# MoE stages with routed experts: units on gathered rows, planned on the core, results added in the stage that follows

## The reference

```python
probs = sigmoid(xt @ gate_w.T + gate_b)
w, idx = top_k(probs, 2)
w = w / (sum(w) + 1e-08)
for e in range(6):
    h = silu(xt @ ew1[e].T) * (xt @ ew3[e].T)
    y = y + ge[:, e:e + 1] * (h @ ew2[e].T)     # ge is w, and zero for four of the six experts
z = silu(xt @ fc1.T) * (xt @ fc2.T) @ fc3.T
x = x + 0.5 * (y + z)                            # xt is layernorm(x)
```

## Time and profile before

| | |
|---|---|
| median of 3 runs | 4698.61 us (4684.21 to 4701.09) |
| the profiled execution | 4671.09 us |
| its span, first to last instruction | 4669.5 us |
| PE, DVE, ACT, POOL busy | 91%, 64%, 49%, 15% |
| mean granted TensorE clock | 0.942 of full |
| moved by DMA | 359.15 MB |

### The profile page before, as it was taken

How to read it: one execution, slowest core, us unless ns; L and a number is a source line. 1 busy time by engine, 2 the same in 40 slices (tenths; PEclk the granted TensorE clock), 3 DMA queues, 4 the chain that set the end, 5 groups by cost and what they waited for, 6 DMA issues and landing times. The chain is left out here.

```text
span 4669.5 us, 79371 instructions
## 1 busy us (share of the span) xinstructions
PE 4239.2 (91%) x25648; PEld 2522.6 (54%) x25648; DVE 3004.6 (64%) x5513; ACT 2295.4 (49%) x4375; POOL 682.8 (15%) x698
## 2 busy tenths in 40 slices
PE   7999969999999999986999989639999999997688
PEld 6888743333333333324888855525656656654454
DVE  5556668888888888835656533746666666663432
ACT  3222317777777777761332222214656556655222
POOL 2232200000000000000233200532222222220000
PEclk9999979999999999987999999868999989998789
DMA  2000172323323322203000000476667667662401
GB/s 85 0 0 0 52 146 38 46 34 43 46 34 44 46 38 39 32 6 120 8 0 0 1 20 0 150 198 179 188 176 184 188 165 186 191 158 52 131 20 36
DMA packets 173944, 359.15 MB, mean 77 GB/s; under 512 B 40586, under 2 KB 104714, under 8 KB 156810
## 3 DMA queue, kind: packets, MB, share of 16 engines
q1 hardware_dynamic: 154634, 304.20, 28.5%
q0 software_dynamic: 18944, 50.35, 3.9%
HBM read 209.71 MB, written 152.06 MB: 77 GB/s over the span
## 5 line engine op out<-in xcount | busy, mean ns | idle before, releaser
L1314 DVE TENSOR_REDUCE full_tops<-psum 128x1 f32<-128x1024 f32 x1024 | 1206.2, 1218 | 184.0 <-PE psum L1218 184.0
L1271 ACT ACTIVATE full_probs<-psum 128x512 f32<-128x512 f32 x2048 | 1065.8, 602 | 299.2 <-PE psum L1190 295.1
L1781 ACT ACTIVATE causal_probs<-psum 128x512 f32<-128x512 f32 (+3 forms) x1280 | 640.2, 533 | 397.9 <-PE psum L1653 230.0
L1190 PE MATMUL psum<-full_q,full_k 49*128 49x512 f32 x2048 | 653.3, 475 | 23.2 <-ACT full_probs L1271 17.2
L1832 DVE TENSOR_REDUCE causal_tops<-psum 128x1 f32<-128x1024 f32 (+7 forms) x704 | 586.8, 857 | 112.6 <-PE psum L1704 112.6
L1190 PEld LDWEIGHTS psum<-full_q,full_k 49*128 49x128 f32 x2048 | 284.5, 186 | 605.8 <-ACT full_probs L1271 576.9
L1199 PE MATMUL psum<-full_probs,full_vh 128*32 128x512 f32 x4096 | 556.8, 616 | 0.7 <-ACT full_probs L1271 0.7
L1218 PE MATMUL psum<-full_k,full_q 48*128 48x512 f32 x2048 | 402.0, 458 | 51.4 <-DMA full_k<-qk_split 23.6
L1653 PE MATMUL psum<-causal_q,causal_k 49*128 49x512 f32 (+3 forms) x1280 | 407.7, 451 | 14.2 <-ACT causal_probs L1781 8.3
L1704 PE MATMUL psum<-causal_k,causal_q 48*128 48x512 f32 (+4 forms) x1152 | 325.3, 414 | 70.2 <-DVE causal_tops L1847 33.4
L274 POOL TENSOR_TENSOR moe_h_lo<-moe_h,moe_h_hi 128x512 fp32r<-128x512 f32 x224 | 290.3, 1296 | 661.2 <-ACT moe_h_hi L387 661.2
(11 more groups left out here) (190 smaller groups left out, 6070.7 us busy)
## 6 DMA issues: line engine op xcount, KB each, us to landing
causal_bias<-bias_tiles SPq DMA_DIRECT2D x32, 1280.0 KB, 6.3
band_scores<-xn POOLq DMA_DIRECT2D x256, 160.0 KB, 4.2
...
```

The lines of the kernel that those rows point to most:

```text
L1190: nc.tensor.matmul(k.psum[:, b, :], k_sb[at, q, kt * P:(kt + 1) * P], q_sb[at, q, n * BLK:(n + 1) * BLK], start=True, stop=True).then_inc( ...
L1271: nc.scalar.activation(pT[:, kt % 4, n * BLK:(n + 1) * BLK], k.psum[:, bank(q, u), :], ACT.Exp).then_inc(p_ready, 1)
L1314: nc.vector.reduce_max(mx[:, q % 2, u // 2, u % 2:u % 2 + 1], src, AX_X).then_inc(m_free, 1)
L1781: nc.scalar.activation(dst, k.psum[:, bank(q, u), 0:(hi - lo) * P], ACT.Exp).then_inc(p_ready, 1)
```

## The change: what it does, and the diff

`moe_then` joins a MoE stage with the stage after it. The MoE stage now has 29 units: for v = 0 to 7 the shared expert on the 8 blocks, then `NX` = 21 units of 512 gathered rows, each of one expert.

- Beside the shared units, DVE chooses two experts a token (`choose`, `weigh`), PE counts with small matmuls how many tokens before this one took the same expert (`positions`), and DVE makes slot numbers of it (`locate`). SP stores the normalized rows to DRAM (`XN`). POOL scatters the token numbers to their slots (`scatter`, 8 indirect DMAs of 128 numbers a block). The gate's matmuls are now float32r parts too.
- After the last block DVE plans the units (`schedule`): for each of the 21 its expert and where its token numbers stand. SP reads the plan and loads weights and numbers of each unit (`load_weights`, `load_ids`); POOL gathers the rows (`gather`, 4 indirect DMAs of 128 rows of 1 KB a unit), four units ahead.
- In an expert unit the rows are transposed and split like x, the weights are split per unit (`split` on ACT, `rest` on DVE), and the result is copied by ACT (`out`) and stored by SP to DRAM (`YS`), not added to x.
- `Returns`: in the following stage POOL gathers for each tile its two result rows per token (`pool_bring`), and DVE adds them with their weights (`dve_add`) ahead of the statistics.
- The first MoE stage no longer waits for all of x; `load_stage` gives each quarter a semaphore and ends with the identity. The loops of the MoE, qkv and LSTM stages that carry new work are unrolled where these need it.

`positions` is six small float32 matmuls a block; `locate` is 13 DVE operations on at most 24 columns, `schedule` 14 on at most 105.

```diff
-STAGES = [moe(0), full_attention, moe(1), lstm(0), causal_attention, lstm(1)]
+ROW_ORDER = list(range(TT))
+PAIR_ORDER = [t * (TT // NB) + n * TB + i for n in range(TT // NB // TB) for t in range(NB) for i in range(TB)]
+STAGES = [moe_then(0, ROW_ORDER, full_attention), moe_then(1, PAIR_ORDER, lstm(0)), causal_attention, lstm(1)]
...
+NX = 16 + E - 1
...
+                def load_weights(b):
+                    if b >= 2:
+                        sp.wait_ge(w_lo, b - 1)
+                    at = sp.value_load(plan[0:1, 0, b:b + 1], min_val=0, max_val=E - 1)
+                    sp.dma_start(w_raw[:, w_slot(NBLK + b), :],
+                                 experts[:, bass.ds(at, 1), :].rearrange("p a x -> p (a x)")).then_inc(s_raw[w_slot(NBLK + b)], 16)
+
+                def load_ids(b):
+                    if b >= 6:
+                        sp.wait_ge(k.gathered[(b - 6) % 4], gathered(b - 6))
+                    at = sp.value_load(plan[0:1, 1, b:b + 1], min_val=0, max_val=HOME - 1)
+                    sp.dma_start(idr[:, b % 6, :], ids[bass.ds(at, 1)].rearrange("a p t -> (a p) t")).then_inc(s_id[b % 6], 16)
+
+                def store(b):
+                    sp.wait_ge(y_copied, 2 * b + 2)
+                    sp.dma_start(outs[b], ybuf[:, b % 2, :, :].rearrange("p t d -> p (t d)")).then_inc(s_y[b % 2], 16)
+
+                sp.wait_ge(plan_ready, 1)
+                for b in range(2):
+                    load_weights(b)
+                sp.wait_ge(k.scattered, scattered_all())
+                for b in range(4):
+                    load_ids(b)
+                load_weights(2)
+                for v in range(NBLK, NV + 1):
+                    if v >= NBLK + 1:
+                        store(v - NBLK - 1)
+                    if v - 5 < NX:
+                        load_weights(v - 5)
+                    if v - 4 < NX:
+                        load_ids(v - 4)
...
+                def scatter(n):
+                    pool.wait_ge(idx_ready, n + 1)
+                    for t in range(n * TB, (n + 1) * TB):
+                        for s in range(2):
+                            pool.indirect_dma_start(
+                                out=k.TOKENS[:, :], out_offset=bass.IndirectOffsetOnAxis(ap=idx[:, s, t:t + 1], axis=0),
+                                in_=token[:, t:t + 1], in_offset=None).then_inc(k.scattered, 16)
+
+                def gather(b):
+                    pool.wait_ge(s_id[b % 6], 16 * (b // 6 + 1))
+                    if b >= 4:
+                        pool.wait_ge(t_ready, 2 * (NBLK + b - 4) + 2)
+                    if b == 0:
+                        for r in range(2):
+                            pool.wait_ge(s_xn[r], 16 * NBLK // 2)
+                    for t in range(TB):
+                        pool.indirect_dma_start(
+                            out=xg[:, b % 4, t, :], out_offset=None, in_=k.XN[:, :],
+                            in_offset=bass.IndirectOffsetOnAxis(ap=idr[:, b % 6, t:t + 1], axis=0)).then_inc(k.gathered[b % 4], 16)
...
+                for v in range(NBLK - 2):
+                    rest(v + 1, 0)
+                    rest(v + 1, 1)
+                    if v + 4 < NBLK:
+                        ln.pool_rstd(pool, v + 4, v % 2)
+                    scatter(v + 1)
+                rest(NBLK - 1, 0)
+                rest(NBLK - 1, 1)
+                scatter(NBLK - 1)
+                for b in range(4):
+                    gather(b)
+                rest(NBLK, 0)
+                rest(NBLK, 1)
+                for v in range(NBLK, NV - 1):
+                    rest(v + 1, 0)
+                    if v - 4 < NX:
+                        gather(v - 4)
+                    rest(v + 1, 1)
...
+                for v in range(NBLK - 2):
+                    up(v + 1, 0, (0,))
+                    positions(v + 1)
+                    up(v + 1, 0, (1,))
+                    transpose(v + 2)
+                    up(v + 1, 1)
+                    gate(v + 2)
+                    down(v, 0)
+                    gate_transpose(v + 2)
+                    down(v, 1)
+                up(NBLK - 1, 0, (0,))
+                positions(NBLK - 1)
+                up(NBLK - 1, 0, (1,))
+                up(NBLK - 1, 1)
+                for v in (NBLK - 2, NBLK - 1):
+                    down(v, 0)
+                    down(v, 1)
+                transpose(NBLK)
+                transpose(NBLK + 1)
+                up(NBLK, 0)
+                up(NBLK, 1)
+                for v in range(NBLK, NV):
+                    if v + 1 < NV:
+                        up(v + 1, 0)
+                    if v + 2 < NV:
+                        transpose(v + 2)
+                    if v + 1 < NV:
+                        up(v + 1, 1)
+                    down(v, 0)
+                    down(v, 1)
...
+                def split(b):
+                    r = w_slot(NBLK + b)
+                    if b >= 2:
+                        act.wait_ge(dn_ready, 2 * (NBLK + b - 3) + 2)
+                    act.wait_ge(s_raw[r], 16 * (b // 3 + 1))
+                    nc.scalar.copy(w_parts[0][:, r, :], w_raw[:, r, :]).then_inc(w_hi, 1)
+
+                def out(b, pair):
+                    act.wait_ge(dn_ready, 2 * (NBLK + b) + pair + 1)
+                    if b >= 2 and pair == 0:
+                        act.wait_ge(s_y[b % 2], 16 * (b // 2))
+                    nc.scalar.copy(ybuf[:, b % 2, 2 * pair:2 * pair + 2, :].rearrange("p t d -> p (t d)"),
+                                   k.psum[:, 4 + pair, :]).then_inc(y_copied, 1)
...
+                for v in range(NBLK, NV):
+                    if v + 1 < NV:
+                        hidden(v + 1, 0)
+                    if v + 2 < NV:
+                        upper_x(v + 2)
+                    if v + 1 < NV:
+                        hidden(v + 1, 1)
+                    out(v - NBLK, 0)
+                    out(v - NBLK, 1)
+                    if v + 3 < NV:
+                        split(v + 3 - NBLK)
...
+                for v in range(NBLK - 2):
+                    locate(v + 1)
+                    hidden(v + 1, 0)
+                    lower_x(v + 2)
+                    if v + 3 < NBLK:
+                        apply(v + 3)
+                    hidden(v + 1, 1)
+                    choose(v + 2)
+                    weigh(v + 2)
+                    update(v)
+                    if v + 4 < NBLK:
+                        stats(v + 4)
+                locate(NBLK - 1)
+                schedule()
+                hidden(NBLK - 1, 0)
+                hidden(NBLK - 1, 1)
+                update(NBLK - 2)
+                rest(1)
+                rest(2)
+                update(NBLK - 1)
+                lower_x(NBLK)
+                lower_x(NBLK + 1)
+                rest(3)
+                hidden(NBLK, 0)
+                hidden(NBLK, 1)
+                address()
+                for v in range(NBLK, NV):
+                    if v + 1 < NV:
+                        hidden(v + 1, 0)
+                    if v + 2 < NV:
+                        lower_x(v + 2)
+                    if v + 1 < NV:
+                        hidden(v + 1, 1)
+                    if v + 3 < NV:
+                        rest(v + 4 - NBLK)
...
+    def pool_bring(self, pool, first, count):
+        k = self.k
+        for i in range(first, first + count):
+            if i >= 8:
+                pool.wait_ge(k.added, self.run * TT + i - 7)
+            g = self.order[i]
+            for s in range(2):
+                pool.indirect_dma_start(
+                    out=self.ring[:, i % 8, s, :], out_offset=None, in_=k.YS[:, :],
+                    in_offset=bass.IndirectOffsetOnAxis(ap=self.back[:, s, g:g + 1], axis=0)).then_inc(k.back[i % 8], 16)
+
+    def dve_add(self, dve, first, count):
+        k, nc = self.k, self.k.nc
+        for i in range(first, first + count):
+            dve.wait_ge(k.back[i % 8], 32 * (self.run * TT // 8 + i // 8 + 1))
+            g = self.order[i]
+            nc.vector.scalar_tensor_tensor(k.X[:, g, :], self.ring[:, i % 8, 0, :], self.wgt[:, 0, g:g + 1], k.X[:, g, :],
+                                           ALU.mult, ALU.add).then_inc(k.added_half, 1)
+        for i in range(first, first + count):
+            dve.wait_ge(k.added_half, self.run * TT + i + 1)
+            g = self.order[i]
+            nc.vector.scalar_tensor_tensor(k.X[:, g, :], self.ring[:, i % 8, 1, :], self.wgt[:, 1, g:g + 1], k.X[:, g, :],
+                                           ALU.mult, ALU.add).then_inc(k.added, 1)
...
             @block.gpsimd
             def _(pool):
+                ret.pool_bring(pool, 0, 2 * TB)
                 ln.pool_rstd(pool, 0, 0)
+                ret.pool_bring(pool, 2 * TB, TB)
                 ln.pool_rstd(pool, 1, 1)
+                ret.pool_bring(pool, 3 * TB, TB)
 
                 def blockwise(n, half, left):
                     if left > 1:
                         ln.pool_rstd(pool, n + 2, half)
-
```

(23 more changed lines are left out.)

713 lines of the change are left out of this document (471 added, 242 removed).

## The result

The change takes 4546.9 us (median of its runs), the kernel before 4694.5: a ratio of 0.968 with a 95% interval of 0.965 to 0.971. It is faster by 3.2%. One of its four executions was a slow one, 5408.2 us at a granted clock of 0.627, which the ratio and its interval leave out. The forecast was 4520 us, with 4400 to 4720 around it.

The account below looks back on a forecast made before the run. The prediction took PE to bound the MoE stages; gains of 221 us there and 7 in the load, less 34 in qkv and 16 in LSTM, make 178: 4698.6 - 178 = 4520 us, range 4400 to 4720.

Parts of the forecast that it names:

- PE stays the bound: MoE stages: a unit takes 9.25 us, a shared block 15; 90 us more gain, 4430 us; chance 0.22.
- The forecast case: Whole kernel: 178 us gained, 4520 us, 4460 to 4600 where this case holds; chance 0.55.
- The ring: Expert units: ACT and DVE wait for each other in fixed order, 10.6 us a unit against PE's 9.25.
- third rival: DVE waits for POOL: each scatter holds a small step; shared block 9 us longer, unit 1; 4744 us, chance 0.10.
- 183 us to the first expert matmul: MoE stage through the joint: 156 + 9.1 + 3 + 3 + 9.1 + 3; after it 5.5 + 212 + 9, and 4 for the clock.
- The 4 us for the slow clock: Joint: PE restarts at 1.2 GHz after its pause; 4 us added, from the LSTM stage's first 24 matmuls against the next.
- The shared block, 18 us: Eight shared blocks: DVE is the bound, 14.9 us of its work plus 3.4 waiting for ACT, 18 us a block.
- 8 scatters 9.1, landing 3: Joint: eight last scatters on POOL at 1.14 us each take 9.1 us, and their landing 3 us.
- the second rival: POOL's price: an indirect DMA costs 2.4 us, POOL bounds MoE, joint and qkv; 239 us more, 4760 us, chance 0.13.
- Weights costed at nothing: Expert units: weight and id loads have two or three units of lead, so they cost 0 us.
- The load: Start of the kernel: the first MoE stage may start on a quarter of X, some 7 us earlier.
- Returned results: Gathering and adding the expert results costs 34 us in the qkv stage and 16 us in the LSTM stage.

Follow-up runs that it names:

- four moves: The change with weight split between first sigmoid and cast, gathers behind both subtractions, scatters ahead of rstd, last block's scatters ahead of its subtractions: 4510.7 us, ratio 0.9628.
- wide rows: The change with token-number rows of 64 bytes, every scattered number written sixteen times side by side: 4569.2 us, a single execution.
- the split moved: The change with an expert unit's weight split placed between the first sigmoid and the cast on ScalarE, one unit later: 4516.7 us, ratio 0.9632.

## Why the prediction was right, and where it was not

- **The bound and the sign.** Right. PE stayed full nowhere in the MoE stages, and its rival "PE stays the bound" is what the four moves reach in the units, 9.25 us. The forecast case held, 4547 us in its range of 4460 to 4600. Nearly all of the gain that is missing, 43 us in the two MoE stages, was lost ahead of the first expert up matmul, which came 26 us late in the first and 18 us in the second.
- **The unit, 10.6 us from a ring.** The ring is right, and moving one link of it took the pitch to 9.25. Its size was made of two errors. Without contention it is 9.9, not 10.6: steps that follow each other on one engine start closer than they last (cast to cast of x 0.52 us for 0.62, copies to split 0.95 for 1.2), and I summed durations. And w_lo takes 3.0 us, not 1.76, beside POOL's subtraction: +1.25, in the place of the 1 us that my third rival gave it. The forecast counted 183 us to the first expert matmul and 231 from there; the trace has 209 (217.14 - 8.0) and 231. The whole miss of the first stage lies ahead of that point. That the second numbers agree is luck: eighteen pitches average 11.0 us, and the last two units, with no up matmuls behind them, end 6.6 and 3.2 us apart where the sum has 10.6 too. The 4 us for the slow clock were about 2 by the trace: eight transposes at 1.97 us for 1.03, and the first five starts of up matmuls in 2.20 us for 1.14 at full pace., from which they were taken, differ by 1.8.
- **The shared block, 18 us.** 19.7. Mis-sized by the term that the third rival named, a DVE step held by POOL, but with another cause: two subtractions at 2.9 us a block, which scatters had pushed there, not one small step a scatter. With them out of the way 16.8 us remain, so my 14.9 + 3.4 was 1.5 too much. By the Trainium skill (SBUF — State Buffer, Who interferes with whom), a DVE instruction with two SBUF inputs contends with a GpSimd instruction that reads SBUF, and the ports that they share are an exclusive lock. By that rule, the trace agrees for w_lo and the choice; x_lo, with one input in PSUM, was never held in the change:

```profile
L671 DVE TENSOR_TENSOR moe_x_lo<-psum,moe_x_hi x116: 678/690/693, 18.0 to 2534.9; 128x512 fp32r<-128x512 f32 x116
```

The three numbers are the least, the median and the greatest duration in ns. The rule was in my hands and weighed at 0.10. The shared blocks lost 2 x 6 x 2.9 = 35 us by it, the units 37; the runs that took it away gained 25 and 39, half of what the change gained.
- **The joint.** The failed step is "8 scatters 9.1, landing 3". POOL's price was near (0.96 + 0.30 us, 1.14 assumed; the second rival, 2.4, is out), and the eight took 11.0 us, the last of them 2.15 beside w_lo. The landing took 12 us and not 3: I took it from DMAs of 160 KB in 64 packets, and none of the rows that I had read from before was of a write so small. The wide rows take it away, so 9 us of the joint are its. The rest of the 26 us: the last choice 4 us later; 5 more until the scatters (an update of 1.3 that the sum left out, the 3.0 in which DVE stood with no releaser on the core, a wait of 1.2 for a sigmoid); the scatters 2; the gathers' landing 7.6 us and not 3, with the loads of two more units' weights beside it (7.7 in the run with wide rows); and 1.6 from there to the first up matmul. "PE has had nothing for some 20 us" became 31.6.
- **Weights costed at nothing.** Right in the steady units of the change, where no split waits for its weights. At the joint they landed after 12 and 23 us instead of 6, but still ahead of the rows: w_lo of unit 1 ends at 196.07 and the first rows are transposed at 210.24. Numbers had the lead for a pitch of 11.2 and not for one of 9.25 (the split moved).
- **The load**, 7 us: 8.6. **Returned results**, 34 and 16: 32.5 in the qkv stage, of which the run without them confirms all. The first qkv matmul came 31.6 us behind the first load of the stage (479.37 - 447.80), 30 forecast, and a block 11.6 us (DVE's statistics at 513.31 and 524.87), 11.7 forecast. At the LSTM the first cell matmul is 37.2 us behind its start (2591.45 - 2554.30) against 20.2 before: 17 for the 16 forecast, and the run without the returns takes it away. The other 4 us there, and the 8.9 of the attention, are within what these stages vary by.
